# A graph network kernel: early reload of the features between two stages, and another order in the preparation

## What is computed

```python
edge_index = jnp.stack([src, dst])
h = jnp.maximum(_layernorm(x, axis=-1), 0.0)
x = x + _L0_gnn_ref(h, src, dst, L0_gnn_W, L0_gnn_a)
h = jnp.maximum(_layernorm(x, axis=-1), 0.0)
x = x + _L1_gnn_ref(h, edge_index, L1_gnn_W, L1_gnn_b)
...
# L0: attention over the edges
h = x @ W
e = s_src[row] + s_dst[col]
e = jnp.where(e > 0, e, ALPHA * e)
e_exp = jnp.exp(e - row_max[row])
...
h_prime = jax.ops.segment_sum(att[:, None] * h[col], row, num_segments=n)
return jax.nn.elu(h_prime)
# L1: three graph convolutions
for l in range(N_LAYERS):
    x_raw = x
    h = x @ W[l]
    agg = jax.ops.segment_sum(h[src] * norm[:, None], dst, num_segments=N) + b[l]
    x = _layer_norm(jax.nn.relu(agg)) + x_raw
```

## Time and profile before

| | us |
|---|---|
| median of 3 runs | 2382.5 (2376.64 to 2386.11) |
| the profiled execution | 2380.24, span in the trace 2378.4 |

### The profile page before, as it was taken

One profiled execution on the slowest core, in us unless ns is written; L12 is line 12 of the kernel. 1 busy time (PEld: TensorE's weight loads), 2 busy tenths in 40 slices (PEclk: granted clock), 3 DMA queues, 4 the chain that ended last, 5 costly groups with the idle time before them and its releaser, 6 DMA issues.

```text
span 2378.4 us, 27767 instructions
## 1 busy us (share of the span) xinstructions
PE 2179.4 (92%) x9986; PEld 1200.1 (50%) x9987; DVE 1016.0 (43%) x2793; ACT 776.1 (33%) x1421; POOL 664.2 (28%) x495
## 2 busy tenths in 40 slices
PE   5799788998789995998999999999999999999998
PEld 4344377555435553454445544564445544555444
DVE  7799989999734455231122121221122111213202
ACT  3577677998723323221111110111111110113100
POOL 3000000101134442433444344433444344440000
PEclk8899955999989997999999999999999999999999
DMA  6200091444321113233222322223222322226582
GB/s 180 71 9 8 13 292 43 149 157 170 119 37 1 14 28 105 40 67 75 26 38 42 71 33 44 35 60 62 26 48 32 74 35 27 27 60 201 209 306 83
DMA packets 185817, 185.51 MB, mean 78 GB/s; under 512 B 110530, under 2 KB 172705, under 8 KB 181740
## 3 DMA queue, kind: packets, MB, share of 16 engines
q1 hardware_dynamic: 119658, 136.95, 18.2%
q0 software_dynamic: 56752, 1.28, 7.0%
q10 hardware_dynamic: 9281, 45.63, 5.3%
HBM read 100.45 MB, written 83.36 MB: 77 GB/s over the span
## 4 chain that ended last, share of the span: by engine, by line
PE 55%; DMA 3%; DVE 1%; issue 0%; ACT 0%; DVEq 0%; ACTq 0%
PE banks L1710 25%; PE banks L1735 21%; PE banks L1832 6%; DMA feat<-hnD 3%; PE banks L1788 1%; PE banks L1696 1%; DMA out_dram<-big 0%; PE banks L1797 0%; PE banks L1850 0%; DVE HN L2003 0%; DVE banks L1998 0%; ACT banks L1895 0%; DVE HN L2000 0%; PE banks L1813 0%; DVE big L2047 0%
## 5 line engine op out<-in xcount | busy, mean ns | idle before, releaser
L882 POOL DMA_INDIRECT WT<-lists x391 | 605.7, 1549 | 855.4 <-DMA WT<-lists 842.2
L1710 PE MATMUL banks<-big,feat 125*128 125x500 f16 (+1 forms) x3150 | 606.2, 353 | 19.9 <-DMA feat<-hnD 15.8
L1710 PEld LDWEIGHTS banks<-big,feat 125*128 125x128 f16 x3150 | 306.3, 97 | 310.0 <-DMA feat<-hnD 16.5
L1735 PE MATMUL banks<-H,U 128*128 128x500 f32 (+1 forms) x756 | 302.6, 541 | 8.7 <-issue 8.7
L1735 PE MATMUL banks<-aT,V 128*128 128x500 f32 (+1 forms) x756 | 296.4, 538 | 3.0 <-DVE HN L2003 3.0
L1735 PEld LDWEIGHTS banks<-aT,V 128*128 128x128 f32 x756 | 143.1, 190 | 145.0 <-issue 97.2
L1735 PEld LDWEIGHTS banks<-H,U 128*128 128x128 f32 x756 | 142.6, 191 | 138.4 <-issue 101.0
L1991 DVE SCALAR_TENSOR_TENSOR HN<-banks,bh,HN 128x500 f32<-128x500 f32 (+1 forms) x70 | 47.8, 683 | 376.2 <-ACT HN L1893 353.8
L1893 ACT ACTIVATE HN<-banks,bs 128x500 f32<-128x500 f32 (+1 forms) x70 | 44.3, 632 | 380.6 <-PE banks L1735 380.6
L1353 PE MATMUL banks<-big,G 125*128 125x500 f16 (+1 forms) x700 | 143.9, 364 | 21.7 <-DVE G L1443 21.7
L1129 PE MATMUL banks<-work 125*128 125x500 f32 (+1 forms) x350 | 153.6, 550 | 10.4 <-ACT work L1070 6.4
(11 more groups left out here) (298 smaller groups left out, 2375.4 us busy)
## 6 DMA issues: line engine op xcount, KB each, us to landing
big<-WT ACTq DMA_DIRECT2D x25, 1562.5 KB, 7.3
WT<-zero SPq DMA_DIRECT2D x39, 980.0 KB, 9.0
hTD<-HN SPq DMA_DIRECT2D x40, 250.0 KB, 2.2
hnD<-stg SPq DMA_DIRECT2D x32, 250.0 KB
feat<-hnD SPq DMA_DIRECT2D x4, 2000.0 KB
H<-hTD SPq DMA_DIRECT2D x16, 500.0 KB, 4.8
work<-xhD SPq DMA_DIRECT2D x28, 250.0 KB
WT<-lists POOLq DMA_INDIRECT x391, 3.0
```

The source lines that it names most:

```text
L882: nc.gpsimd.indirect_dma_start(out=WT, out_offset=bass.IndirectOffsetOnAxis(ap=lists[:, 0, t - first:t - first + 1], axis=0), in_=lists[:, ...
L1710: last = nc.tensor.matmul(SUMS[s % 2][half][:, 0:wid(ch)], rows_, A[:, j, cols(ch)], start=(j == 0 and part == 0), stop=(j == T - 1 and pa ...
L1735: last = nc.tensor.matmul(PS[bank][:, 0:w], wt_[:, kt, g:g + 128], v[:, kt, 0:w], start=(n == 0), stop=(n == len(terms) - 1))
```

## The change

Four things are done.

1. In prepare, ScalarE's queue issues the second half of x ahead of the near-edge list, and not behind it.
2. In prepare, VectorE makes the list `tli` and splits the edges' weights (`wp`) first, and takes all 25 statistics after both, ahead of the use of the gathered tiles.
3. One allocation `room` ([128, 2, 3200] f32) holds `trow`, the edges' columns and later `feat`; buffers of attention move within it and within `work`. When the last logit is made, SyncE reloads tiles 0 to 21 of the normed rows into `room` (three loads, `GROUPS`). ScalarE writes those of the last chunk, tiles 22 to 24, straight to their place; they are not stored to `xh1D` any more.
4. At the end of attention SyncE waits neither for the last store of x1 nor for one of the normed rows. Convolutions waits for the x1 stores ahead of L1302, loads nothing at its start, and waits on the semaphores `landed`, which both blocks share.

```diff
+        landed = [sem("early_" + n) for n in ("a", "b", "c", "d", "x1_out")]
+        room = kept("room", [128, 2, T * D])
+        trow = room[0:P + 1, 0, 0:N]
...
+        feat = room[0:P].rearrange("p h n -> p (h n)").bitcast(f16).rearrange("p (t a d) -> p t a d", a=2, d=S2)
...
+                act.dma_start(xn[:, XA:T], xt[:, XA:T]).then_inc(x_in, 16)
                 act.wait_ge(dve_did, EDGES)
                 act.dma_start(nearD.rearrange("(g t e) o -> t g (e o)", g=EG, t=LANE), near1[:]).then_inc(cs_out, 16)
-                act.dma_start(xn[:, XA:T], xt[:, XA:T]).then_inc(x_in, 16)
...
-                def spread(lo, hi):
-                    for j in range(lo, hi):
-                        V_.bn_stats(stats[:, j, :], xn[:, j, :])
-                dve.wait_ge(x_in, 32)
-                spread(0, 5)
                 dve.wait_ge(red_r, 1)
...
-                spread(5, T - 1)
-                done(V_.bn_stats(stats[:, T - 1, :], xn[:, T - 1, :]))
                 dve.wait_ge(edge_c, EG)
...
+                dve.wait_ge(x_in, 32)
+                for j in range(T):
+                    last = V_.bn_stats(stats[:, j, :], xn[:, j, :])
+                done(last)
...
+GROUPS = ((0, 0, 2 * NQ), (1, 2 * NQ, 4 * NQ), (2, 4 * NQ, FIRST[SC - 1]))
...
+        early = room[0:P, 0, :].rearrange("p (t d) -> p t d", d=D)
+        spare = room[:, 1, :]
+        half = spare[0:P, 0:2 * CH].rearrange("p (h n) -> p h n", h=2)
+        PT = spare[0:P, 2 * CH:2 * CH + TB].rearrange("p (r n) -> p r n", r=RP)
...
+                sp.wait_ge(l_r, len(unit_list))
+                for s_, lo, hi in GROUPS:
+                    sp.wait_ge(xh_out, 16 * (CHUNK[hi - 1] + 1))
+                    sp.dma_start(early[:, lo:hi, :], xh1D[:, lo:hi, :]).then_inc(landed[s_], 16)
                 stores(SC - 1)
-                normed(SC - 1)
-                sp.wait_ge(x1_out, 16 * SC)
-                sp.wait_ge(xh_out, 16 * SC)
                 sp.wait_ge(zeros, 16 * ZF)
...
                     act.wait_ge(rs_r, ch + 1)
+                    end = ch == SC - 1
                     for q in range(rows[ch]):
-                        last = nc.scalar.activation(y[:, q, :], t[:, q, :], ACT.Relu, bias=rs[:, 3, q:q + 1], scale=rs[:, 1, q:q + 1])
-                    last.then_inc(xh_r, 1)
+                        last = nc.scalar.activation(early[:, FIRST[ch] + q, :] if end else y[:, q, :], t[:, q, :], ACT.Relu,
+                                                    bias=rs[:, 3, q:q + 1], scale=rs[:, 1, q:q + 1])
+                    last.then_inc(landed[3] if end else xh_r, 1)
...
-                for s_, lo, hi in groups:
-                    sp.dma_start(xr[:, lo:hi], xh1D[:, lo:hi]).then_inc(s_, 16)
-
                 sp.wait_ge(agg_r, B0)
+                sp.wait_ge(landed[4], 16 * SC)
                 sp.dma_start(x2, x1D).then_inc(x1_in, 16)
...
-                    for s_, lo, hi in groups:
+                    for s_, lo, hi in GROUPS:
                         if lo == ch * NQ:
-                            act.wait_ge(s_, 16)
+                            act.wait_ge(landed[s_], 16)
+                    if ch == FIRST[SC - 1] // NQ:
+                        act.wait_ge(landed[3], 1)
```

## The result

| | before | changed |
|---|---|---|
| median of 6 runs each, us | 2380.6 (2376.6 to 2386.1) | 2359.5 (2355.7 to 2360.8) |
| ratio, 95% interval | 1 | 0.9912 (0.9901 to 0.9922) |
| profiled execution, us | 2380.2 | 2359.3 |
| its span, us | 2378.4 | 2357.5 |

What follows compares the result with a forecast made beforehand. The prediction took TensorE (55% of the span, chain starting in the recurrent layers) as the bound. Gains of 7.4 us in prepare and 11.0 from attention to convolutions, 18.4 in all, gave 2364.1 us against 2382.5; range 2356 to 2373.

Steps and rivals of the forecast that it cites:

- List at 29.5, first indirect load at 30: Prepare: VectorE's tile list ends at 29.5 us, not 40.03; GpSimd's first indirect load starts at 30, between 29.8 and 36.
- Tiles by 38.4, L605 at 39.6: Prepare: gathered tiles land by 38.4 us; VectorE starts using them at 39.6, not 48.73, 9.1 earlier.
- Weights 1.1 later: Prepare: x's second half, moved ahead of the weights, delays them by 0.13 MB at 115 GB/s, 1.1 us.
- rival A: Prepare: weights come late, 4.8 us taken, second load awaited beyond 35; gain there 3.7, time 2368; 15%.
- Cap 7.1 less the delay: Prepare: ScalarE's features until 64.20 cap its first copy's gain at 7.1 us; less the weights' 1.1, 6.0.
- Clock 1.4: Prepare: without idle time four TensorE matmuls run at full clock, half their 2.77 us, gaining 1.4 us.
- Barrier 0.72, then 0.83: End of attention: barrier costs 0.72 us, ScalarE's two weight issues 0.83 more; features first scaled at 653.92, not 660.74.
- Reload covered: Attention to convolutions: SyncE issues at about 640.6, all lands by 655 to 657; tile 16 needed at 659, 2 us cover.
- 14.5 us for the first aggregate: Start of convolutions: 50 TensorE matmuls, 6 us of work at half clock, take 14.5 us, ending at 670.9, not 681.92.
- place two: From attention to the convolutions, where TensorE idles 19.01 us: a gain of 11.0 us, 9.4 to 12.2 by the clock.
- rival B: Attention to convolutions: the reload comes no earlier or lands late, only the wait's 3.0 us is gained; 2372; 8%.
- Rival C: Attention: sharing one allocation slows VectorE's 175 logits; 0.105 us more each cancels the gain, 0.2 gives 2399; 3%.

Runs made afterwards that it cites:

- reload_late: Changed kernel with the three reloads issued at the start of convolutions, attention's end waiting for the normed rows' stores ahead of it: 2371.4 us, ratio 0.9951.
- warm: Changed kernel plus 34 unused TensorE matmuls at the end of attention and 13 at the start of convolutions: 2368.7 us, ratio 0.9955.
- weights_first: Changed kernel with SyncE asking for both folding weights ahead of its first half of x: 2359.5 us, ratio 0.9906.
- waits_kept: Changed kernel with SyncE's waits for the residual store and the reload kept at the end of attention: 2365.7 us, ratio 0.9939.
- after_again: The changed kernel run once more, unaltered, on a second chip: 2362.6 us, ratio 0.9919.
- tail_only: Changed kernel with both prepare orders (ScalarE's queue, VectorE's statistics) put back: 2372.8 us, ratio 0.9951.

## Why the prediction was right

The direction, the two places and the mechanism at each were right, and the sum of 18.4 was 2.6 below the 21.0 that the profiles show. By its own steps:

- **List at 29.5, first indirect load at 30.** Measured 29.51 and 30.39. That it came so near 30 is in part luck: the list's store landed 23.4 us after its issue, at 29.5, together with the list, and I had given it anything up to 36. The load starts 0.9 behind it; without the new order on ScalarE's queue (x_behind) it starts 0.3 behind VectorE, at 29.84. In four other kernels with that order the store is what GpSimd waits for, in reload_late longest:

```profile
31.16 1.70 POOL L316 DMA_INDIRECT big<-nearD,big  x1 [8.15 <-DMA nearD<-big]
```

- **Tiles by 38.4, L605 at 39.6.** The 25 statistics ended at 38.9 and the tiles were awaited until 39.76, a wait of 0.63. They came 9.4 us after the first load's start, where I had said 8.4 at most. Most of that isn't the issuing: the four loads' issues ended 5.44 us after their start against 5.24 before. Each took 4.5 us in the median from issue to landing and not 3.5, while the weights moved beside them (221 GB/s from 28 to 40 us, against 115 from 38 to 50 before); that the weights are the cause is argued, not shown. The first load took 1.52 us beside the casts, not 1.29, but 1.29 again in warm, beside the same split. So the rule of the Trainium skill (SBUF — State Buffer, two separate sides) is borne out by 0.2 us at most; it had been given up to 4.6.
- **Weights 1.1 later.** Measured 2.12 (33.04 against 30.92), and 1.94 at the folding's end. This term was mis-sized: I priced x's bytes by a row of the queue's tail, but SyncE's issue was held 13.92 us, 4.4 longer than before, so the first weights came 4.25 later, and only the second ones' own idle time (2.94 to 0.80) gave 2.1 back. Against rival A I had said that bytes only change places. They don't: both halves of x drained at 97 GB/s together, where the first had most of 98 before, and with 0.37 of the engines' time. The weights, which with nothing of x ahead of them brought the engines to 221 GB/s and a share of 0.83 (weights_first, 4 to 8 us), couldn't be issued meanwhile. That is rival A's mechanism at its half size; its threshold of 35 wasn't reached.
- **Cap 7.1 less the delay.** ScalarE's first copy moved 5.24 us, to 66.05, right behind its affine: 7.1 - 1.94 = 5.2.
- **Clock 1.4.** Measured 7.64 - 5.24 = 2.4. Not only the four matmuls but all from 70.14 to 77 us ran at half clock before, the transposes between ScalarE's copies too; I counted one row of it. The two misses nearly cancel: 7.4 forecast, 7.64 measured.
- **Barrier 0.72, then 0.83.** The first issue came 0.27 behind the last affine's end (643.99), the scaling 1.25 behind it (645.24), and not 1.55. The 0.72 held SyncE's issue of the last store (0.25) and 0.45 from the end of its wait to the first issue; the changed kernel has neither.
- **Reload covered.** No wait for a DMA in all 25, and the issue came where I put it: 632.25, which is 640.6 less the 8.4 by which attention's end came earlier. The 115 GB/s, taken from a row of another stage, were near enough (129 measured in waits_kept), and what I had left out were bytes: the rest of the normed store ahead, and the residual store, which I had put behind the reload and which landed before it. The last packets came by 649.0, which with the 8.4 is 657.4, against 655 to 657; tile 16 was due at 658.4 and not 659. The cover was 1 us (0.6 in after_again) and not 2.
- **14.5 us for the first aggregate.** 13.2: half clock lasted 4.2 us of work, not 6. The three bounds I gave (3.5, 6, 9.9) held it; I took the middle. With the barrier this is place two's 1.6 us more (12.6 against 11.0).
- **Parts within place two.** I gave 3.0 to the wait and the rest to the reload. The experiments split it as 5.5 to 5.8 for the block's end with the last tiles in place and 6.2 to 7.1 for the early reload; rival B's 3.0 was therefore too low.
- **Rival C.** A logit takes 602 ns in the mean for 375 columns, as before, and 733 against 734 for 500. False.
- **What I did not see.** The scatters. I wrote that all behind a place moves if nothing else is late, and did not ask what runs from one block to the next. GpSimd's stream of 391 scatters does. Before, its last started at 2145.38 and ScalarE's reader at 2167.60, 22 us apart; in the changed kernel 7, in its repeat 15. Where the reader waited, it came 6.6 (waits_kept), 8.5 (warm) and 9.0 us (tail_only) behind the last start. So in the changed kernel's profile the gain just fitted in; that it did is luck, for the stream's length alone differs by up to 24 us between profiles, more than the two gains together.

## What to carry to other kernels

A gain at an early stage is worth its time only up to the slack of the streams that run past that stage: before pricing a restart, list each chain that spans several blocks and how far its last piece lies ahead of its reader, and shift its work into an engine's stand if that is small. Where a queue serves small lists and large arrays, price the order by what is held behind the large one, its issue too, and not by bytes alone. That the DMA engines are busy doesn't mean that bytes only change places: look at the share of them that is used. A wait for a whole transfer at a block's end costs more than its readers would: they need its first piece first, and let each wait for its own.

## What the runs showed of the hardware

- An issue on a queue can hold its engine for long: 11.94 us for the list's store behind 0.77 MB of features on ScalarE's queue, 13.92 for the weight load behind x's first half on SyncE's, and 20.13 in weights_first for w_hh behind it. In the changed kernel ScalarE's first copy moved from 8.76 to 19.34 by that, and it cost nothing only because TensorE had no weights until 29.41; in weights_first it did set TensorE's start.
- The arrays of 125 rows moved with a third of the DMA engines' time: the reload at 129 GB/s and a share of 0.32 with nothing beside it, both halves of x at 97 GB/s and 0.37. With the weights (128 rows) beside them it was 262 GB/s from 20 to 24 us.
- The granted clock after an idle stretch of 11.9 us was 0.51 for the first 4.2 us of the next stage's work, and 1.00 after 7.35 and 2.93 us of needless matmuls in that stretch: 50 matmuls took 10.75 us and not 12.77. In the six profiles with this code and a stand of 11.9 to 12.9 us they took from 12.13 to 13.62.
- Small operations on ScalarE and VectorE stood 1 to 4 us between 46 and 62 us, released by nothing that the profile names ("remote", "issue"), with the same code: in no profile of the second chip, and in those of the other two. What it is stays open; no run took away one of the transfers beside it.
- The chained scatters (1.55 us each to issue, some 3.3 apart in the median) took 1189 to 1212 us for 317 of them and 1195 to 1220 for 321: a spread of 25 us that decides whether they are late. 32 to 44 gaps of over 5 us in each profile make part of it: of the 24 us between before and warm, 12 are in such gaps.
